# Two decay tiles ahead of a SiLU on ScalarE in a state-space stage

## The reference

```python
zxbcdt = x @ w_in.T
z, xs, Bs, Cs, dt = jnp.split(zxbcdt, ...)
xBC = silu(causal_conv4(concat([xs, Bs, Cs])) + conv_b)     # 6 channel tiles of 128
dt = softplus(dt + dt_bias); A = -exp(A_log); a = dt * A
cs = cumsum(a)                                              # within a token tile
Ldec = where(tri, exp(cs[:, None] - cs[None, :]), 0)        # the decays
att = (Cc @ Bc.T) * Ldec
Y = att @ (Xc * dt) + D * Xc
y = (Y * silu(z)) @ w_out.T
```

## Time and profile before

| what | us |
|---|---|
| median of 3 runs | 990.43 |
| lowest, highest | 989.28, 991.11 |
| the profiled execution | 990.58 |
| its span, first to last instruction | 988.4 |
| TensorE busy in the span | 948.0 (96%) |
| ScalarE busy in the span | 486.6 (49%) |

### The profile page before, as it was taken

The page is one execution under the profiler, slowest core; times in us unless marked ns, Lnnn a source line. Parts: engine busy times, 40 slices in busy tenths (PEclk is TensorE's granted clock), DMA queues, the critical chain, the costliest instruction groups (busy, mean ns, idle before and its releaser), DMA issues.

```text
span 988.4 us, 15661 instructions
## 1 busy us (share of the span) xinstructions
PE 948.0 (96%) x4926; PEld 785.0 (79%) x4926; DVE 638.7 (65%) x1421; ACT 486.6 (49%) x1358; POOL 524.1 (53%) x432
## 2 busy tenths in 40 slices
PE   5998999999999999989999999999999999999895
PEld 3766688878888888878888888888888888888782
DVE  5745553422312257888768778778768778778877
ACT  5756442322231246645645644654645645555554
POOL 4336533743433456864575574673673763854323
PEclk9999999999999999999999999999999999999997
DMA  6200123310111111010110110110110120110002
GB/s 221 86 1 1 42 62 112 107 64 0 64 64 64 43 65 35 23 43 22 44 44 22 43 53 11 42 53 11 42 54 10 42 64 0 43 53 12 1 1 85
DMA packets 18024, 45.69 MB, mean 46 GB/s; under 512 B 2176, under 2 KB 2816, under 8 KB 16704
## 3 DMA queue, kind: packets, MB, share of 16 engines
q1 hardware_dynamic: 17984, 45.20, 13.8%
HBM read 43.10 MB, written 2.10 MB: 46 GB/s over the span
## 4 chain that ended last, share of the span: by engine, by line
PE 75%; POOL 8%; DVE 7%; issue 4%; ACT 2%; DMA 2%; SPq 0%; POOLq 0%; DVEq 0%; ACTq 0%
PE bank L511 22%; PE bank L512 21%; PE bank L513 21%; PE bank L828 4%; POOL w_lo L1580 2%; PE bank L838 2%; DMA raw_a<-in_w_q 2%; DVE pb L2299 1%; POOL pb L1837 1%; POOL res L1698 1%; PE bank L522 1%; POOL raw_a L1742 1%; PE bank L815 1%; DVE bst L2129 1%; PE bank L572 1%
## 5 line engine op out<-in xcount | busy, mean ns | idle before, releaser
L511 PE MATMUL bank<-act_hi,w_hi 128*128 128x512 f32 x448 | 183.6, 410 | 1.6 <-DVE act_lo L1942 1.6
L512 PE MATMUL bank<-act_lo,w_hi 128*128 128x512 f32 x448 | 175.6, 392 | 0.0
L513 PE MATMUL bank<-act_hi,w_lo 128*128 128x512 f32 x448 | 175.5, 392 | 0.0
L1837 POOL TENSOR_TENSOR pb<-pb,prec 128x512 f32<-128x512 f32 x64 | 66.8, 1044 | 163.2 <-DVE prec L2308 163.2
L1580 POOL TENSOR_TENSOR w_lo<-raw_a,w_hi 128x512 fp32r<-128x512 f32 x101 | 130.2, 1301 | 37.1 <-ACT w_hi L1302 21.6
L1371 ACT ACTIVATE pb<-pb,nmax 128x128 f32<-128x128 f32 x256 | 99.4, 391 | 46.5 <-DVE nmax L2303 46.4
L511 PE MATMUL bank<-w_hi,ot_hi 128*128 128x512 f32 x256 | 106.2, 415 | 1.1 <-DVE ot_lo L1942 0.6
L1580 POOL TENSOR_TENSOR h_lo<-hb,h_hi 128x512 fp32r<-128x512 f32 x28 | 37.4, 1336 | 120.5 <-ACT h_hi L1243 120.5
L511 PEld LDWEIGHTS bank<-act_hi,w_hi 128*128 128x128 f32 x448 | 84.9, 190 | 20.5 <-issue 4.4
L513 PE MATMUL bank<-w_hi,ot_lo 128*128 128x512 f32 x256 | 100.5, 393 | 0.0
L512 PE MATMUL bank<-w_lo,ot_hi 128*128 128x512 f32 x256 | 100.2, 391 | 0.0
(11 more groups left out here) (233 smaller groups left out, 2328.3 us busy)
## 6 DMA issues: line engine op xcount, KB each, us to landing
raw_a<-in_w_gu SPq DMA_DIRECT2D x7, 1024.0 KB, 5.3
raw_a<-in_w_q SPq DMA_DIRECT2D x28, 256.0 KB, 3.3
raw_b<-in_w_kv SPq DMA_DIRECT2D x8, 512.0 KB, 3.3
raw_b<-in_w_dn SPq DMA_DIRECT2D x7, 512.0 KB, 3.5
raw_b<-in_w_o SPq DMA_DIRECT2D x7, 512.0 KB, 5.0
raw_a<-in_w_o SPq DMA_DIRECT2D x14, 256.0 KB, 4.0
res<-in_x SPq DMA_DIRECT2D x8, 256.0 KB, 6.1
raw_b<-in_ctx_t SPq DMA_DIRECT2D x8, 256.0 KB, 3.0
```

Of the source, the lines that this page charges most:

```text
L511: mm(o, l_hi, r_hi, start=first, stop=False)
L512: mm(o, l_hi, r_lo, start=False, stop=False)
L513: return mm(o, l_lo, r_hi, start=False, stop=last)
L1837: TT(pb[:, jj % 2, :, :], pb[:, jj % 2, :, :], prec[:, jj % 2, :].unsqueeze(2).to_broadcast([P, GH, L]), ALU.mult).then_inc(p_norm, 1)
```

## The change

On ScalarE's queue alone, one call moves. Before, the SiLU of channel tile 7 stands ahead of x and the decays of token tile 2; after, it stands behind the decays of token tile 3, right ahead of the SiLU of channel tile 8. The x copies and decays of tiles 2 and 3, the split of y of tile 0 and the copy of projection step 12 so all move one place ahead.

```diff
             decay(1)
             conv_silu(6)
             in_evac(11)
-            conv_silu(7)
             x_evac(2)
             decay(2)
             y_split(0)
             in_evac(12)
             x_evac(3)
             decay(3)
+            conv_silu(7)
             conv_silu(8)
             in_evac(13)
             y_split(1)
```

## The result

The changed kernel takes 988.5 us at the median (986.11 to 989.93, 20 runs), the kernel before, timed in turn with it, 990.52 (988.81 to 991.49, 20 runs). The medians lie 2.0 us apart. The ratio of the timed runs is 0.9977 with a 95% interval of 0.9971 to 0.9983: 2.3 us faster, with 1.7 to 2.9 in the interval. The forecast was 987.7 and 2.7 us; the range 985.5 to 989.5 holds the median, the narrower range of its outcome A alone (987.1 to 988.3) does not.

A forecast was written before the change was run, and what follows sets the result against it. TensorE, busy 96% of the span, was taken as the bound. VectorE's round, starting 2.68 us sooner, set the gain, other terms adding nothing: 990.58 to 987.9 profiled, 987.7 from the 990.43 median; range 985.5 to 989.5.

The forecast's parts named there:

- outcome A: The forecast: the 2.13 us gap ahead of ssm2(3) stays, the clock falls behind it; 987.7 (987.1 to 988.3), chance 0.53.
- early decays of tile 2: On ScalarE, the decays of token tile 2 are ready at about 68.0 instead of 71.32, 3.3 us sooner.
- The round on VectorE, 4.70 us: From att_mul(2) to ssm2(2), 4.70 us as before, so att_mul(2) starting 2.68 us sooner gains that (2.4 to 3.0).
- The second round and the gap of 2.13 us: VectorE's round from ssm2(2) to ssm2(3) stays 5.98 us, so TensorE's 2.13 us gap ahead of ssm2(3) stays.
- Table loads: On ScalarE, two loads before and after, 1.28 us each, counted at 0.
- Slack behind the move: On ScalarE, SiLU 7 comes 5.5 us later unharmed; in_evac(13) ends at 75.4, conv(9) wants it at 77.6, cover 2.2 us.
- Rival C: On ScalarE's queue, in_evac(13) comes too late for conv(9); fully lost gain gives 990.4; chance 0.18 with partial losses.
- The clock: TensorE's clock fall between ssm2(3) and cum_step(5) costs about 1.5 us, had back only if the clock doesn't fall.
- B: The clock does not fall behind the gap ahead of ssm2(3); gain 4.15 us, 986.3; chance 0.25.
- Rival D: Slower: TensorE's clock falls at more places, about 1.5 us each; four more give 993.7; chance 0.04.
- The sum: The 2.68 us gain set by VectorE's round, taken off the whole kernel's time: 987.7 from the median of 990.43.

The follow-up runs named there:

- e_pool: Changed kernel with decay_in(4) and decay_in(5) behind decay_out(3) and ahead of y_rest(1) on GpSimd's queue; median 988.9 us, ratio 0.9987 to the kernel before.
- e_pool2: Changed kernel with GpSimd waiting for att_mul(2) and att_mul(3), so it stands still beside both L2035; median 986.58 us, ratio 0.9961.
- e_mid: Changed kernel with the SiLU of channel tile 7 right behind decay(2), half the move, two more table loads; median 989.25 us, ratio 0.9989.
- after_again: The changed kernel as it is, timed again beside other kernels; 988.92 us in 11 runs, ratio 0.9983 to the kernel before.
- e_ahead: Changed kernel with cum_step(4) and in_step(15) moved ahead on TensorE, ScalarE and GpSimd reordered to follow; median 983.93 us, ratio to before 0.993.

## Why the prediction was right, and where it was off

*Faster by the early decays of tile 2.* Right in place and mechanism. ScalarE's copy at 65.20 (forecast 65.28), decays ready at 67.94 (68.0), `cum_step(3)` at 69.64 (69.7), `att_mul(2)` at 69.94 (70.02), released by TensorE.

*The round on VectorE, 4.70 us.* This is the term that was off. It took 75.06 - 69.94 = 5.12 us, because L2035 took 1.46 and not 1.03. I gave 1.33 as the most that GpSimd can do to it, from one row where GpSimd was busy throughout; that was no bound, and the old trace itself has an L2035 of 1.35 (at 111.88). What decides is when GpSimd's instruction ends (last section). So `ssm2(2)` came 2.26 us sooner against `ssm2(1)` instead of 2.68, outside the 2.4 to 3.0 given for this round, and the gap ahead of it was 0.68 us instead of 0.2. e_pool and e_pool2 show the cause by taking it away.

*The second round and the gap of 2.13 us.* Right: 5.99 us for 5.98, gap 2.12.

*Table loads.* Two as before. The first exponential starts 1.30 us after its load starts (65.50 to 66.80), as in the earlier trace rows; with the 2.66 us of the Trainium skill's page "ScalarE: Activation LUTs" (section "What ACT_TABLE_LOAD costs") the gain would by the forecast's estimate have been 1.9 us. The further 1380 ns of that page are not seen here.

*Slack behind the move.* Right: `in_evac(13)` ended at 75.65, wanted by `conv(9)` at 78.02. SiLU 7 came 5.4 us later (73.42 against 68.07), as the forecast's own times give (73.5 - 68.07), where its text says 5.5. Rival C, ScalarE giving the gain back, did not come. e_mid shows that the slack also holds two more table loads.

*The clock.* The price was right: 1.47 forecast, 1.46 measured. The fall comes and goes in both kernels, so that A and B are not two outcomes but a mixture in the runs of either; the forecast only touched on that. The changed kernel's first profile took B's course. Rival D did not come. The timed ratios give 2.3 and, in after_again, 1.7 us, on both sides of the 2.25 at equal clock. How close the first of them comes is in part luck, since it hangs on how many executions of each kernel had a fall, here and at 425 us. And the stated range holds the median by the room that it gave to C: with 0.4 us less of gain and this mixture, 988.5 lies outside A's own 987.1 to 988.3.

*The sum.* 2.68 forecast, 2.25 in the trace at `ssm2(3)`, 2.3 (1.7 to 2.9) in the timed runs.

## What to carry to other kernels

When a queue in strict order waits, look at what stands behind the waiting instruction and is ready; then follow the moved work on to the first round that another engine sets, since that round and not the closed gap is the gain. A move on one engine shifts what runs side by side on two others: here 0.43 of 2.68 us went to that, and up to `ssm2(3)` it came back by moving GpSimd's work away from VectorE's instruction with two SBUF inputs. Filling a gap with work from behind (e_ahead) gave more here than making one shorter. And where executions of one kernel differ by more than the change is worth, compare the distance between two instructions around the change, and not the spans.

## What the runs showed of the hardware

L2035 reads two tiles in SBUF; L2033, the convolution and `y_out` read one and a bank of PSUM. Of these only L2035 was stretched by GpSimd, and GpSimd's own instruction was stretched in turn when it came second. GpSimd in the kernel before, beside the L2035 of the earlier trace rows that starts at 73.42 and ends at 74.45:

```profile
72.62 1.28 POOL L1580 TENSOR_TENSOR y_lo<-yb,y_hi 128x512 fp32r<-128x512 f32 x1
73.86 1.49 POOL L1628 TENSOR_TENSOR md<-dt_sb,tris 128x512 f32<-128x512 f32 x1
```

`y_rest(0)` began first and took its usual 1.28 us, to 73.90; L2035 ended 0.55 us later. `decay_in(4)` has a start at 73.86 but took 1.49 us in place of 1.04, as if begun at 74.31, about when L2035 was done. In the changed kernel `decay_in(4)` (70.52) began 0.14 us ahead of L2035, kept its 1.04 us and ended at 71.56; L2035 ended at 72.12, 0.56 us behind it. In e_pool `y_rest(1)` ended at 79.32 and L2035 at 79.87, again 0.55. The longest L2035 of the old trace, and the GpSimd instruction that it started beside:

```profile
111.88 1.35 DVE L2035 TENSOR_TENSOR att<-att,diag_d 128x512 f32<-128x512 f32 x1
```

```profile
111.39 1.29 POOL L1633 TENSOR_TENSOR em<-em,md 128x512 f32<-128x512 f32 x1
```

GpSimd ended at 112.68, L2035 at 113.23. In all 13 profiles every L2035 that started while a GpSimd instruction ran ended 0.54 to 0.56 us behind that instruction, and took 0.71 to 1.67 us; every other one took 0.69. So of the two instructions one runs and the other waits, and the one that started first goes first. The Trainium skill says this (page "SBUF — State Buffer", section "SBUF: two separate sides"): VectorE with two SBUF inputs and GpSimd take the same ports in turn, each for a whole instruction. The traces agree.

The old trace already had the 0.55 us. With the forecast's own times an estimate of the stretch was possible before the run: `decay_in(4)` from about 70.6 (68.07 and two GpSimd instructions of 1.27), which is just ahead of L2035 at 70.74; ended 1.04 later, at 71.65; L2035 ended at 72.2. That is about 1.5 us for it, where 1.46 was measured.

The clock of TensorE: behind the gaps of 1.59 and 1.10 us of the old order, and of 1.74 in e_pool2, it stayed at its upper level in every profile; behind gaps of 2.1 to 2.6 us ahead of `ssm2(3)` it fell to the lower one in 4 of 9 (2.13, 2.11, 2.13 and 2.61 us fell; 2.12 three times, 2.13 and 2.46 did not). From `ssm2(3)` to `cum_step(5)` that cost 1.5 us in three of them and 1.2 in e_mid. Behind the wait of 2.54 to 2.56 us for `qpart` near 425 us it fell in 11 of 13.
